# A graph layer on one core: rows that SP and ScalarE fetched one by one are gathered by POOL

## What is computed

```python
seg = edge_dst * r + edge_type
S   = segment_sum(h[edge_src], seg, n * r).reshape(n, r, d)     # rows of x, summed per node and type
cnt = segment_sum(ones, seg, n * r).reshape(n, r)
agg = einsum('nrd,rdf->nf', S, relation_weights) + cnt @ rFeatures
h   = relu(agg * norm + (agg * norm) @ loop_weight)             # norm = degree ** -0.5
x   = layernorm(x + h)
```

## Time and profile before

| | |
|---|---|
| median of 3 runs | 1577.52 us (1574.93 to 1591.05) |
| profiled execution, span from the first to the last instruction | 1576.6 us |
| PE busy | 1049.6 us, 67% |
| DVE busy | 732.7 us, 46% |
| ACT busy | 528.4 us, 34% |
| POOL busy | 798.1 us, 51% |
| mean granted clock of PE | 0.853 |

### The profile page before, as it was taken

The page is one execution under the profiler, slowest core; times in us unless marked ns, Lnnn a source line. Parts: engine busy times, 40 slices in busy tenths (PEclk is TensorE's granted clock), DMA queues, the critical chain, the costliest instruction groups (busy, mean ns, idle before and its releaser), DMA issues.

```text
span 1576.6 us, 31507 instructions
## 1 busy us (share of the span) xinstructions
PE 1049.6 (67%) x6713; PEld 931.1 (59%) x6713; DVE 732.7 (46%) x2573; ACT 528.4 (34%) x1119; POOL 798.1 (51%) x822
## 2 busy tenths in 40 slices
PE   1388777847774768474687486746576657774868
PEld 0277667736763668464576375635565546664758
DVE  5464555525452545243455254534354525552545
ACT  2353333323332334232343133323243313331433
POOL 7536565626562556353555264636364635562650
PEclk9989998969796888687998798968798979877989
DMA  6623332313231323131333132313132312231320
GB/s 200 215 62 89 90 92 77 93 45 91 77 91 46 87 78 88 48 91 44 88 87 89 45 84 70 95 46 89 54 88 70 91 51 83 82 88 46 86 77 22
DMA packets 71124, 127.58 MB, mean 81 GB/s; under 512 B 18417, under 2 KB 44002, under 8 KB 70930
## 3 DMA queue, kind: packets, MB, share of 16 engines
q0 software_dynamic: 37920, 102.48, 22.9%
q1 hardware_dynamic: 17698, 16.04, 3.3%
q10 hardware_dynamic: 15312, 7.01, 1.6%
HBM read 115.86 MB, written 9.60 MB: 80 GB/s over the span
## 4 chain that ended last, share of the span: by engine, by line
SPq 58%; issue 33%; PE 3%; DMA 0%; DVE 0%; ACT 0%; DVEq 0%; ACTq 0%
SPq L526 50%; SPq L523 8%; PE agg_ps L1160 1%; PE win_ps L1148 1%; PE win_ps L1233 1%; DMA x_parts<-x_out 0%; DMA x_out<-x_parts 0%; PE win_ps L1186 0%; ACT ring L692 0%; PE win_ps L1130 0%; PE win_ps L1237 0%; PE win_ps L1185 0%; DVE h_sb L935 0%; DVE y_sb L939 0%; DVE y_mid L945 0%
## 5 line engine op out<-in xcount | busy, mean ns | idle before, releaser
L572 POOL DMA_INDIRECT rows<-x_parts,src x756 | 745.8, 986 | 717.9 <-PE win_ps L1148 414.4
L692 ACT COPY ring<-win_ps 128x451 f32 x831 | 465.4, 560 | 948.5 <-PE win_ps L1148 420.1
L1160 PEld LDWEIGHTS agg_ps<-ring,w 128*128 128x128 f32 x3936 | 619.6, 210 | 106.4 <-issue 56.5
L1160 PE MATMUL agg_ps<-ring,w 128*128 128x128 f32 x3936 | 629.8, 294 | 45.0 <-issue 44.1
L1148 PE MATMUL win_ps<-hot,rows 128*128 128x480 f32 x1614 | 595.9, 457 | 12.3 <-issue 10.0
L1028 DVE TENSOR_TENSOR ring<-ring,win_ps 128x41 f32 x831 | 187.1, 225 | 808.2 <-ACT ring L692 606.2
L896 DVE TENSOR_SCALAR hot<-iota,key_f 128x480 fp32r<-128x480 f16 x831 | 393.7, 474 | 3.7 <-issue 3.7
L1148 PEld LDWEIGHTS win_ps<-hot,rows 128*128 128x128 f32 x1614 | 271.6, 210 | 14.7 <-issue 10.2
L1130 PE MATMUL win_ps<-hot_node,hot_type 128*128 128x12 bf16 x831 | 87.3, 172 | 214.9 <-DVE ring L1028 109.9
L1130 PEld LDWEIGHTS win_ps<-hot_node,hot_type 128*128 128x128 bf16 x831 | 70.9, 103 | 262.1 <-issue 215.1
L1148 PE MATMUL win_ps<-hot,x_out 128*128 128x480 f32 x48 | 24.1, 597 | 230.2 <-DMA x_out<-x_parts 227.4
(11 more groups left out here) (94 smaller groups left out, 259.7 us busy)
## 6 DMA issues: line engine op xcount, KB each, us to landing
x_out<-x_parts SPq DMA_DIRECT2D x2314, 1.0 KB
rows<-x_parts,src POOLq DMA_INDIRECT x756
x_out<-x_parts ACTq DMA_DIRECT2D x640, 1.0 KB
x_parts<-x_out SPq DMA_DIRECT2D x6, 512.0 KB
x_parts<-ring SPq DMA_DIRECT2D x6, 512.0 KB
out<-out_sb ACTq DMA_DIRECT2D x48, 64.0 KB
x_blk<-x ACTq DMA_DIRECT2D x47, 64.0 KB
w<-relation_w SPq DMA_DIRECT2D x8, 320.0 KB
```

The source lines that it names most:

```text
L572: pool.indirect_dma_start(rows[0:n, k].rearrange("p c d -> p (c d)").bitcast(F32), None, x_parts, bass.IndirectOffsetOnAxis(ap=src[0:n, t: ...
L692: nc.scalar.copy(ring[:, :, bass.ds(start + 1, WIN - 1)], win_ps[bank_of(t)][:, :, 1:WIN]).then_inc(copied, 1)
L1160: ins = nc.tensor.matmul(sums_of(c), w[:, r, :], ring[:, r, bass.ds(seg, BLOCK)], start=(r == 0), stop=(r == COLS - 1))
```

## The change

BY_ROW and BY_ACT, SP's loop over rows, ACT's fetch, the index tables with their loads and conversions, and their semaphores are taken out. POOL gathers every tile with its indirect DMA, and PE waits for gathered[k] in all of them.

```diff
-ROW_TILE = 6
-BY_ROW = [(6 + j * 41 // 17) * TPB + ROW_TILE for j in range(18)] + [-(-E // P) - 1]
-BY_ROW_BUFS = 6
-ACT_FROM = 4
-ACT_ROWS = 1
-ACT_BLOCKS = 8
-ACT_TILE = 12
-BY_ACT = [i * TPB + ACT_TILE for i in [*range(ACT_FROM + ACT_BLOCKS, BLOCKS - 1, ACT_BLOCKS)]]
...
         def gathers_into(k, t):
 
-            return len([n for n in range(k, t + 1, TPB) if n not in BY_ROW and n not in BY_ACT])
+            return len(range(k, t + 1, TPB))
...
-            sp.wait_ge(by_row_cleared, 1)
-            for j, t in enumerate(BY_ROW):
-                of = src_by_tile[t:t + 1, :] if t < FULL else src_rest.rearrange("p o -> o p")
-                sp.dma_start(by_row_src[j:j + 1, 0:rows_in_tile(t)], of).then_inc(by_row_src_loaded, 16)
             sp.wait_ge(pos_done, 1)
             sp.dma_start(pos[:].rearrange("o (b k) -> o b k", k=POS)[:, :, 0:TPB], pos_2d[:, 0:TPB]).then_inc(pos_ready, 16)
...
-                for j, t in enumerate(BY_ROW):
-                    if j >= BY_ROW_BUFS:
-                        sp.wait_ge(tile_done, BY_ROW[j - BY_ROW_BUFS] + 1)
-                    for first in range(0, rows_in_tile(t), ROW_LOAD):
-                        ps = range(first, min(first + ROW_LOAD, rows_in_tile(t)))
-                        index = [sp.alloc_register(f"sp_row{j}_{p}") for p in ps]
-                        sp.load(index, by_row_at[j:j + 1, ps[0]:ps[-1] + 1])
-                        for p, reg in zip(ps, index):
-                            at = sp.snap(reg, donate=True)
-                            sp.dma_start(by_row[p:p + 1, j % BY_ROW_BUFS].rearrange("p c d -> p (c d)").bitcast(U8),
-                                         x_bytes[:, bass.ds(at, ROW_BYTES)]).then_inc(by_row_landed[j], 16)
...
             def gather(t):
-                if t in BY_ROW or t in BY_ACT:
-                    return
                 k = t % TPB
...
                         nc.scalar.copy(ring[:, :, bass.ds(start + 1, WIN - 1)],
                                        win_ps[bank_of(t)][:, :, 1:WIN]).then_inc(copied, 1)
-                        fetch(i, k)
...
-                dve.wait_ge(act_src_loaded, 16)
-                nc.vector.tensor_scalar(act_at[:], act_src[:], float(ROW_BYTES), None, ALU.mult).then_inc(act_ready, 1)
-                dve.wait_ge(by_row_src_loaded, len(BY_ROW) * 16)
-                nc.vector.tensor_scalar(by_row_at[:], by_row_src[:], float(ROW_BYTES), None, ALU.mult).then_inc(by_row_ready, 1)
...
-                    if t in BY_ROW:
-                        pe.wait_ge(by_row_landed[BY_ROW.index(t)], rows_in_tile(t) * 16)
-                    elif t in BY_ACT:
-                        pe.wait_ge(by_act_landed[BY_ACT.index(t)], P * 16)
-                    else:
-                        pe.wait_ge(gathered[k], gathers_into(k, t) * 16)
+                    pe.wait_ge(gathered[k], gathers_into(k, t) * 16)
```

More of the change, by code:

```diff
@@ L38 @@
 POS_LOAD = 4
-ROW_LOAD = 32
 ROUND_SHIFT = 10
@@ L71 @@
 PLAIN = PLAIN_BLOCKS * TPB
-ROW_TILE = 6
-BY_ROW = [(6 + j * 41 // 17) * TPB + ROW_TILE for j in range(18)] + [-(-E // P) - 1]
-BY_ROW_BUFS = 6
-ACT_FROM = 4
-ACT_ROWS = 1
-ACT_BLOCKS = 8
-ACT_TILE = 12
-BY_ACT = [i * TPB + ACT_TILE for i in [*range(ACT_FROM + ACT_BLOCKS, BLOCKS - 1, ACT_BLOCKS)]]
-ACT_BUFS = 2
-ACT_LOAD = 4
-ROW_BYTES = 2 * D * 4
 X_ROWS = N // P
@@ L105 @@
 assert 8 * (STAGE_BUFS - X_BUFS) <= 2 * COLS and 2 * D <= 2 * SEG
-assert ACT_ROWS * ACT_BLOCKS * TPB >= P and P % ACT_LOAD == 0 and BY_ACT[-1] < FULL and not set(BY_ACT) & set(BY_ROW)
 assert USED > LAST * TPB + SUMS_FROM and R % W_LOAD == 0 and FREE_W % W_LOAD == 0
@@ L130, in bank_of, with build @@
     return BANK_OF["tile", t]
-def build(nc, x, src_main, src_by_tile, src_rest, dst_main, dst_rest, type_main, type_rest, r_features, relation_w, loop_w, out):
+def build(nc, x, src_main, src_rest, dst_main, dst_rest, type_main, type_rest, r_features, relation_w, loop_w, out):
     with ExitStack() as ctx:
@@ L199, in build @@
         x_out = sb("x_out", [P, 2, STAGE, PARTS, D], F32R)
[L200 to L206, removed]
         hot = sb("hot", [P, HOTS, R * WIN], F32R)
@@ L288, in build @@
         gather_issued = sem("gather_issued")
[L289 to L295, removed]
         gathered = [sem(f"gathered{k}") for k in range(TPB)]
@@ L352, in gathers_through @@
         def gathers_through(t):
-            return t + 1 - len([n for n in BY_ROW + BY_ACT if n <= t])
+            return t + 1
         def group_of(t):
@@ L455, in _ @@
                 sp.dma_start(t[0:REST, FULL:FULL + 1], rest).then_inc(edges_loaded, 16)
-            sp.dma_start(act_src[:], src_by_tile[BY_ACT[0]:BY_ACT[-1] + 1:ACT_BLOCKS * TPB, :]).then_inc(act_src_loaded, 16)
             def stage_load(n):
@@ L512, in in_order @@
                         w_load((n - 3) * W_LOAD)
[L513 to L516, removed]
-                for j, t in enumerate(BY_ROW):
-                    if j >= BY_ROW_BUFS:
-                        sp.wait_ge(tile_done, BY_ROW[j - BY_ROW_BUFS] + 1)
-                    for first in range(0, rows_in_tile(t), ROW_LOAD):
-                        ps = range(first, min(first + ROW_LOAD, rows_in_tile(t)))
-                        index = [sp.alloc_register(f"sp_row{j}_{p}") for p in ps]
-                        sp.load(index, by_row_at[j:j + 1, ps[0]:ps[-1] + 1])
-                        for p, reg in zip(ps, index):
-                            at = sp.snap(reg, donate=True)
-                            sp.dma_start(by_row[p:p + 1, j % BY_ROW_BUFS].rearrange("p c d -> p (c d)").bitcast(U8),
-                                         x_bytes[:, bass.ds(at, ROW_BYTES)]).then_inc(by_row_landed[j], 16)
-                        for reg in index:
-                            sp.free_register(reg)
             def g_load(t):
@@ L646, in _ @@
             regs = [act.alloc_register(f"act_pos{k}") for k in range(TPB)]
[L647 to L670, removed]
             def step(i, tiles, sums, late, fin):
@@ L822, in stage_low_part @@
                 nc.vector.tensor_tensor(low_part, of, high_part.bitcast(F32), ALU.subtract).then_inc(stage_low, 1)
-            nc.vector.memset(by_row_src[:], 0).then_inc(by_row_cleared, 1)
             nc.vector.memset(zeros[:], 0.0).then_inc(zeros_done, 1)
@@ L1132, in tile @@
                 if not known_less(i, PLAIN_BLOCKS) or not isinstance(i, int):
-                    if t in BY_ROW:
-                        pe.wait_ge(by_row_landed[BY_ROW.index(t)], rows_in_tile(t) * 16)
-                    elif t in BY_ACT:
-                        pe.wait_ge(by_act_landed[BY_ACT.index(t)], P * 16)
-                    else:
-                        pe.wait_ge(gathered[k], gathers_into(k, t) * 16)
+                    pe.wait_ge(gathered[k], gathers_into(k, t) * 16)
                 elif k % 2 == 0:
                     pe.wait_ge(low_done, i * GROUPS + k // 2 + 1)
[L1141 to L1146, removed]
+                of = rows[:, k]
                 for part in range(PARTS):
@@ L1294 @@
         arrays[f"{name}_main"] = np.ascontiguousarray(a[:FULL * P].reshape(FULL, P).T)
-        if name == "src":
-            arrays["src_by_tile"] = np.ascontiguousarray(a[:FULL * P].reshape(FULL, P))
         arrays[f"{name}_rest"] = np.ascontiguousarray(a[FULL * P:].reshape(REST, 1))
```

## The result

| | before | after |
|---|---|---|
| median of 4 runs each on the same chip | 1582.24 us (1574.93 to 1591.05) | 1362.43 us (1355.92 to 1364.2) |
| profiled execution: span | 1576.6 us | 1359.0 us |
| mean granted clock of PE | 0.853 | 0.908 |

The ratio is 0.8595, with a 95% interval of 0.8552 to 0.8638: the kernel is 14% faster. The forecast was 1286 us, so the time is 76 us above it. It misses the forecast's own band (1235 to 1315) and lies in rival 1's (1315 to 1370), which the range took in whole.

What follows compares the result with a forecast made beforehand. The prediction took SP's queue of row DMAs, 1.94 us a tile, as the bound. From the 1576.6 us span it summed −227 − 63 + 0 − 5 + 4 to 1285.6, forecast 1286 us, range 1170 to 1370.

Steps and rivals of the forecast that it cites:

- the forecast's own band: The likeliest case, around the summed time of 1286 us: 1235 to 1315 us; chance 0.50.
- rival 1: Only the 227 us wait goes; ScalarE's loss is hidden or the clean pace luck: 1348 us, 1315 to 1370; chance 0.23.
- The first term: SP's 2314 row DMAs go, and with them PE's 227.4 us of waits for x_out: −227 us.
- The second term: ScalarE's 640 row DMAs between its copies go: 0.093 us for each of 680 tiles, −63 us.
- the prediction's last sentence: Wrong if PE's pauses without a cause depend on SP (faster) or come with the density of gathers (slower).
- POOL's 24 gathers: 24 more gathers take 31 us of POOL's time, covered by its 414 us of waiting for PE: 0.
- The prologue: Without SP's 19 index loads pos can be issued 14 us earlier: −5 us, ends 0 and −17.
- The tail: Of the last 26 tiles, done at 1.2 us each, the first 15 now go at the ordinary pace: +4 us.
- Rival 2: POOL becomes the bound at 1.286 us a gather as PE's pauses vanish with SP: 1138 us, 1130 to 1235; chance 0.20.
- Rival 3: Gathers get dearer with VectorE busier: at 1.69 us each 1451 us, with half that increase 1296; chance 0.05.
- Rival 4: Slower: POOL's descriptor work as only row source; sign turns at 1.85 us a gather, 2.0 gives 1695 us; chance 0.02.
- The clock: PE's granted clock was to rise from 0.85 to 0.9 or more.

Runs made afterwards that it cites:

- experiment 5: The changed kernel again, without edit, on held chip 0: 1360.7 us against 1588.08 for the kernel before, ratio 0.8571.
- experiment 6: The kernel before again, without edit, for its trace on held chip 0: 1577.83 us in one run.
- experiment 11: Kernel before with only SP's row DMAs removed, ACT's five tiles kept, on held chip 6: 1350.82 us against 1551.17, ratio 0.8696.
- experiment 12: Changed kernel with every second gather left out from tile 102, on held chip 6: 996.79 us against the kernel before's 1551.17, ratio 0.6417.
- experiment 2: Kernel before with only ACT's row DMAs removed, SP's 19 tiles kept, on free chip 13: 1056.76 us against 1053.66, ratio 1.0033.
- experiment 1: Kernel before with only SP's row DMAs removed, ACT's five tiles kept, on free chip 13: 1071.85 us against 1053.66, ratio 1.0178.
- experiment 3: Changed kernel with every second gather left out from tile 102, on free chip 13: 944.25 us, ratio 0.8966 to the kernel before.
- experiment 4: Changed kernel with no gathers from tile 102 on, on free chip 13: 944.56 us, ratio 0.8969 to the kernel before.
- experiment 7: The changed kernel, without edit, on free chip 7: 1076.66 us against 1052.44 for the kernel before, ratio 1.0237.
- experiment 8: Kernel before with only SP's row DMAs removed, ACT's five tiles kept, on free chip 7: 1070.53 us, ratio 1.0179.
- experiment 9: Changed kernel with every second gather left out from tile 102, on free chip 7: 945.74 us, ratio 0.8993 to the kernel before.
- experiment 10: Kernel before with 10 tiles on SP in place of 19, ACT's five kept, on free chip 7: 1062.7 us, ratio 1.0105.

## Why the prediction was right, and where it was wrong

**The first term, −227, was right.** The stalls for x_out went whole, no wait for gathered rows came in their place, and the sign and most of the size follow. It holds for held chips; on a free one nothing waits for SP.

**The second term, −63, is the step that failed; it measured about +8.** Counted from the tile that ACT copies: tile 51 at 123.6 us before and 124.4 after, tile 830 at 1555.1 and 1337.2, the end at 1576.6 and 1359.0. The difference of the spans, −217.6, is 0.8 up to tile 51, −218.7 between, of which −227.4 are the stalls and 0.5 the tail, and 0.3 behind tile 830. That leaves +8.2 for everything else. The second pair of traces (experiments 5 and 6) leaves more: −213.6 between tiles 51 and 830, of which −231.5 are stalls, so some +18. A gain of 63 is in neither. The step had two faults.

*The pace of the "clean" stretch was luck: one stretch of 51 tiles is too short.* I took 74.7 us for 51 tiles from PE's restart to its stop, 1.465 us a tile. But PE restarts with six free banks and stops ahead of the others, by a lead that varies. ACT's copies in the trace of the kernel before, at tile 754 and at tiles 802, 803 and 804:

```profile
1439.72 0.54 ACT L692 COPY ring<-win_ps 128x451 f32 x1 [23.43 <-PE win_ps L1148]
...
1510.48 0.54 ACT L692 COPY ring<-win_ps 128x451 f32 x1 [0.17 <-issue]
1511.27 0.27 ACT L735 COPY fin_sb<-win_ps 128x129 f32<-128x129 f32 x1 [0.25 <-issue]
1516.63 0.54 ACT L692 COPY ring<-win_ps 128x451 f32 x1 [5.09 <-remote]
1517.34 0.59 ACT L692 COPY ring<-win_ps 128x451 f32 x1 [0.17 <-ACT ring L692]
```

The copy of tile 754 starts 2.9 us behind the start of its matmuls, that of tile 804 (1517.34) 7.1 us behind (1510.21). From copy to copy the 50 tiles take 77.6 us, **1.552** each. The long stretch by copies, 270.48 to 1359.02 us for 577 tiles less 188.0 of stalls, gives 1.561. By that reading the difference that the term rests on is 0.009 us and not 0.093, 680 tiles give −6, and the sum is 1343.

But this reading is no firmer than the first. The copies come in bunches, and with an end two tiles earlier, at the copy of tile 802 (1510.48), the same stretch gives 1.474 us a tile; with ends at tiles 795 to 804 it gives 1.47 to 1.57. In the changed kernel, stretches of 51 tiles between tiles 100 and 800 take 1.47 to 1.68 us a tile by PE's starts, 1.566 in the median, and 1.47 to 1.69 by the copies; less than 1% of those by PE's starts are under 1.48, and none is as short as 1.465. So the stretch was one of the shortest that there are, and 0.093 us is what such stretches differ by without any change. The trace of before gave no ground for the term, and none for a firm 6 either.

*The waits that "thin out together" were taken for a loss of time.* ACT's row DMAs did make its copies late and PE wait for the ring add; both shrank as forecast. Between tiles 68 and 800 PE's waits for the add fell from 99.4 to 38.9 us and its unexplained pauses grew from 114.3 to 168.7; experiment 11 shows the same exchange backwards with ACT's rows kept, at no cost in time that its interval shows. Something slower stood behind both.

**What it was: the prediction's last sentence, not its forecast.** It would be wrong, it said, "if they come with the density of gathers (then slower)". Experiment 12 shows that on a held chip they do. My ground for setting it aside, that the gathers come hardly denser than between the stalls, was true, and beside the point: the pauses were there already between the stalls, at 1.56 us a tile, and they stayed. Rival 1's time was right, and of its two reasons the first ("hidden by something else") and the second ("clean pace were luck") hold.

**POOL's 24 gathers, 0, was right where it was made.** POOL still stands for PE. With PE no longer held, on free chips, the cover is gone and they cost 24.2 us; the prediction put 31 on that case.

**The prologue, −5, measured +0.8 here, and not the same everywhere.** ACT's timeline in the changed kernel, against its 39.32:

```profile
23.87 0.41 ACT L589 CAST rows<-raw 128x256 fp32r<-128x256 f32 x1 [3.57 <-DMA pos<-w]
24.40 0.54 ACT L615 COPY ring<-win_ps 128x451 f32 x1
```

pos landed 15 us earlier, as forecast, and the first copy started at 24.4. But in this pair tile 51 was not reached any earlier; in that of experiments 5 and 6 it came 4.3 us earlier (120.5 for 124.8). On free chips ACT copies tile 51 at 89.4 us with SP's 19 index loads (experiment 2) and at 85.4 to 86.1 without them (1, 3, 4, 7, 8 and 9): there the term is −3 to −4, near the forecast. On a held chip two executions of one kernel differ there by as much as the term (124.4 and 120.5).

**The tail, +4, measured 0.5:** tiles 805 to 830 took 29.1 us before and 29.6 after. So the buffers filled during the last stall had been worth next to nothing.

**Rival 2** (1138 us, POOL as the bound, pauses gone with SP) was wrong for this chip, since the pauses never hung on SP, and its bound is right for the other kind, at 1077. **Rival 3:** a gather took 986 ns in the mean before and 984 after, so no. **Rival 4** had its mechanism right and its point from a held chip: 1.85 us a gather there, 1.22 on a free one.

**The clock** rose to 0.908, as said. It follows the pauses: 0.84 in the long stretch before, 0.90 after, 1.00 in experiment 12, where PE never stood, and 1.00 in the same window of experiment 7, where it was busy for 631.1 of 681.6 us.

## What to carry to other kernels

When a pace is read from a short stretch, move its ends by a few tiles and read it at two engines before a term rests on it: here 51 tiles gave 1.465 us by PE's starts and anything from 1.47 to 1.57 by ACT's copies, and the term of 63 us was a difference of 0.093. When two waits shrink and the time per unit doesn't, look for what paces both by thinning out the suspected supply (experiment 12) rather than by removing what waits. And before tuning a balance between engines, see whether the chip shows the pauses at all: the same edit is 14% faster on one and 2.4% slower on another, and no version tried here beats both kernels on both kinds; 19 tiles on SP are the best of these on a free chip, none on a held one, with or without ACT's five, which the runs don't tell apart (the middle way of experiment 10 wasn't tried there).

## What the runs showed of the hardware

**Two kinds of chips.** One program took 1052 to 1054 us on two chips and 1551 to 1588 on two others. The amount of DMA traffic alone isn't it: the changed kernel moved 113 GB/s in the window of a free chip, without a pause, and 90 on a held one. A packet of a gather took 159 ns in the median on both. The hold isn't PE's alone: of SP's 2314 row DMAs 12% took over 0.65 us in the kernel before, against a median of 0.224, and none did on a free chip (0.330 at the longest, experiment 2). The queue that bound the kernel before, 0.62 us a row in place of 0.39, was itself a held one. And time is lost ahead of the gathers from x_parts too: the changed kernel issued the first of them at 100.7 us on a held chip and at 71.9 on a free one, and reached tile 51 at 124 and at 86.

**On a held chip PE's completions arrive in bunches.** ACT's timeline in the changed kernel at tiles 802 to 804, and PE's:

```profile
1301.50 0.54 ACT L615 COPY ring<-win_ps 128x451 f32 x1 [0.17 <-issue]
...
1306.10 0.54 ACT L615 COPY ring<-win_ps 128x451 f32 x1 [3.89 <-remote]
1306.81 0.59 ACT L615 COPY ring<-win_ps 128x451 f32 x1 [0.17 <-ACT ring L615]
```

```profile
1301.28 1.15 PE L1055 MATMUL win_ps<-hot,rows 128*128 128x480 f32 x2
...
1302.93 1.01 PE L1055 MATMUL win_ps<-hot,rows 128*128 128x480 f32 x2
```

Tile 803's pair ends at 1302.43 by PE's records, and ACT waits for nothing but its tile_done. The events of that semaphore, read from the trace, come at 1305.99 and 1306.15, 0.16 us apart, though a tile takes PE 1.07 us when nothing keeps it (experiments 3 and 9), and the copy starts 0.1 us behind the first. From 268 to 900 us, 28% of the intervals between the tile_done events on record (about half of the 831) are under 0.3 us in the changed kernel, 29% in the kernel before; in experiments 7 and 12 none is. That is, as far as these tiles show, what "remote" hides in the 364 us of ACT's waits: the copies wait up to 6.5 us for such events, the ring adds wait for the copies, and PE with six banks waits for the adds. It fits the exchange seen in experiment 11. Whether the matmuls themselves end late, or only word of them, the records don't tell, and what in a held chip does this stays open. No run separates the gathers' number from their bytes, or from POOL's work to issue them, either.

**The port shared by DVE and POOL** stays a small thing. The gathers took 886, 949 and 1524 ns (least, median, longest) in the changed kernel and 884, 946 and 1430 on the free chip, where DVE's tiles come a quarter denser (one in 1.25 in place of 1.57 us). Behind this measurement: the Trainium skill (SBUF — State Buffer, "SBUF: two separate sides") advises issuing from ScalarE or SP for the sake of that port. On the free chips the advice is right by 24 us, but because POOL's queue is full, and the port's share isn't visible in the median. The prediction read the longest gathers as the port's. Most follow the kind of chip: 20% of the gathers took over 1 us before and 19% after, but 2% on the free chip, where DVE is the busier. In experiment 9, with half the gathers and a tile every 1.07 us, it is 12%; what of that is the port's, no run separates.
